# Expert blocks of a transformer layer with scaled float16 high and low parts in place of float32 ones

## The reference

```python
q, k, v = x @ Wq, x @ Wk, x @ Wv                    # 16 heads of 64
a = softmax(q k^T / 8) v;  x = layernorm(x + a @ Wo + bo)
logits = (softmax(q'[:, None] * k'[None, :]) * v').sum()   # 8 experts, q', k', v' = x @ wqkv.T
top 2 of 8 experts per token, weights = softmax of the two logits
h1 = x @ w1[e].T; a, g = split(h1); he = silu(a) * g @ w2[e].T     # a, g: 352 wide
x = layernorm(x + sum of weight * he over the token's two experts)
```

## Time and profile before

| | us |
|---|---|
| median of 3 runs | 823.8 (823.46 to 823.82) |
| the profiled execution | 824.94 |
| its span, first to last instruction | 823.0 |
| PE busy | 761.4 |
| ACT busy | 703.2 |
| POOL busy | 650.7 |
| DVE busy | 532.5 |

### The profile page before, as it was taken

The page is one execution under the profiler, slowest core; times in us unless marked ns, Lnnn a source line. Parts: engine busy times, 40 slices in busy tenths (PEclk is TensorE's granted clock), DMA queues, the critical chain, the costliest instruction groups (busy, mean ns, idle before and its releaser), DMA issues. The chain is left out here.

```text
span 823.0 us, 22272 instructions
## 1 busy us (share of the span) xinstructions
PE 761.4 (93%) x9183; PEld 522.9 (64%) x9183; DVE 532.5 (65%) x836; ACT 703.2 (85%) x941; POOL 650.7 (79%) x416
## 2 busy tenths in 40 slices
PE   1899999999999999999999999999999987999991
PEld 0346565666666666666666666666665656899990
DVE  6857666666666666666686766776666678653453
ACT  3799998989898989899999999998989995566672
POOL 5788897878787878788899878999999981267741
PEclk9999999999999999999999999999999999899995
DMA  5602139303030303030304040404030015113312
GB/s 182 157 2 45 38 72 160 73 11 77 7 69 15 71 12 78 5 79 6 78 5 113 5 114 5 116 2 116 3 82 8 11 34 122 45 40 98 108 40 90
DMA packets 42930, 49.30 MB, mean 60 GB/s; under 512 B 6577, under 2 KB 27447, under 8 KB 42704
## 3 DMA queue, kind: packets, MB, share of 16 engines
q1 hardware_dynamic: 39664, 43.31, 22.4%
q0 software_dynamic: 2496, 4.24, 1.6%
q10 hardware_dynamic: 672, 0.33, 0.2%
HBM read 14.28 MB, written 9.25 MB: 29 GB/s over the span
## 5 line engine op out<-in xcount | busy, mean ns | idle before, releaser
L909 POOL TENSOR_TENSOR pl<-p,ph 128x1024 f16<-128x1024 f32 x242 | 511.4, 2130 | 72.0 <-ACT ph L805 71.8
L972 DVE TENSOR_REDUCE mx<-mps 128x1 f32<-128x1024 f32 x249 | 303.9, 1221 | 132.8 <-PE mps L637 130.6
L804 ACT ACTIVATE p<-sps,escale 128x1024 f32<-128x1024 f32 x256 | 287.4, 1123 | 43.4 <-PE sps L617 36.6
L805 ACT ACTIVATE ph<-sps,escale 128x1024 f16<-128x1024 f32 x256 | 286.2, 1118 | 0.0
L715 PE MATMUL pair_bank<-v,ph 128*128 128x65 f16 x2048 | 214.5, 193 | 5.0 <-DVE ao L1012 4.3
L715 PEld LDWEIGHTS pair_bank<-v,ph 128*128 128x128 f16 x2048 | 190.8, 96 | 39.8 <-DVE pl L976 4.1
L717 PE MATMUL pair_bank<-v,ph 128*128 128x64 f16 x2048 | 214.3, 195 | 0.0
L719 PE MATMUL pair_bank<-v,pl 128*128 128x65 f16 x2048 | 213.9, 192 | 0.0
L717 PEld LDWEIGHTS pair_bank<-v,ph 128*128 128x128 f16 x2048 | 190.0, 97 | 29.0 <-issue 0.2
L616 PE MATMUL sps<-q_hh,k_hl 128*128 128x512 f16 x512 | 194.9, 381 | 3.4 <-ACT ph L805 3.1
L617 PE MATMUL sps<-q_lm,k_h 65*128 65x512 f16 x512 | 195.4, 382 | 0.0
(11 more groups left out here) (249 smaller groups left out, 971.0 us busy)
## 6 DMA issues: line engine op xcount, KB each, us to landing
q_hh<-work SPq DMA_DIRECT2D x60, 128.0 KB, 2.3
k_hl<-work SPq DMA_DIRECT2D x58, 128.0 KB, 2.5
q_lm<-work SPq DMA_DIRECT2D x30, 128.0 KB, 2.4
k_h<-work SPq DMA_DIRECT2D x30, 128.0 KB, 2.5
sorted<-pad SPq DMA_DIRECT2D x1, 2990.0 KB, 17.8
xb<-sorted SPq DMA_DIRECT2D x46, 65.0 KB, 2.1
v<-in_w1T SPq DMA_DIRECT2D x8, 352.0 KB, 3.7
v<-home SPq DMA_DIRECT2D x4, 512.0 KB, 4.5
```

The costliest lines, as they stand in the source:

```text
L804: nc.scalar.activation(p32[:, n % 4, :], sps[:, n % 2, :], ACT.Exp, bias=EXP_BIAS, scale=escale[:, 0:1])
L805: nc.scalar.activation(ph[:, n % 4, :], sps[:, n % 2, :], ACT.Exp, bias=EXP_BIAS, scale=escale[:, 0:1]).then_inc(s_exp, 1)
L909: nc.gpsimd.tensor_tensor(pl[:, n % 4, :], p32[:, n % 4, :], ph[:, n % 4, :], ALU.subtract).then_inc(s_subp, 1)
L972: nc.vector.tensor_reduce(mx[:, i // TB, i % TB:i % TB + 1], src, AX.X, ALU.max).then_inc(s_mx, 1)
```

## The change

The token rows, the gated middle rows and both expert weights are held as a float16 high part and a float16 low part, scaled by fixed units and by the weights' greatest values. Where before tokens and w1 were fp32r halves and the middle rows and w2 plain float32, now all are float16 pairs:

- **Greatest values.** SP loads w1 a second time, as 128 long rows (`w1_raw`), at the end of its part for pair 0, into the tail of the values' tile, and w2 (`w2_raw`) at the end of pair 3. VectorE reduces them in twelve pieces of 704 columns at the slots of `WEIGHT_TOPS`, the first eight waiting for w1_raw. The column of ones in tiles 10 to 15 of the values is set after that. Two jobs are added, `wtop` at (8, 0) and `wspread` at (8, 15), by which the values reach all partitions, and VectorE derives five units from them (seven small instructions).
- **w1, w2.** High parts by ScalarE with a scale, low parts by VectorE as scale times value minus high. w2 is loaded in pair 13; its three high parts are made at ScalarE's start of the mixture, its three low parts (1024 columns each) on VectorE behind `split_block(3)`.
- **Middle rows.** They are cut in 117, 117 and 118 in place of 128, 128 and 96. ScalarE makes the high part of all 384 columns in one instruction; VectorE makes the low part from the bank. `down` has nine float16 products of 128 columns.
- **Order.** ScalarE's `take_hidden(i - 1)` stands ahead of `take_block(i + 2)`; VectorE's `low_hidden(i - 1)` stands between `gated(i)` and `split_block(i + 2)`.
- Rows are scaled by 2048 when they are copied, and the units are taken out in the silu's scale and in the tokens' weights (one more small instruction in `total`). `bo` lies in a part of `ao`. The second batch's value tiles are made tile by tile.

```diff
+WEIGHT_TOPS = {(0, 13): 0, (0, 14): 1, (1, 1): 2, (1, 2): 3, (1, 6): 4, (1, 10): 5, (1, 11): 6, (1, 14): 7,
+               (4, 2): 8, (4, 6): 9, (4, 10): 10, (4, 14): 11}
+FRONT_JOBS = {(8, 0): ("wtop", 0), (8, 15): ("wspread", 0), (9, 15): ("turnx", 0), ...
-F_CHUNKS = [(0, 128), (128, 128), (256, 96)]
+F_CHUNKS = [(0, 117), (117, 117), (234, 118)]
...
@@ sync, in the loop over pairs, behind spread_head @@
+                if pp == 0:
+                    sp.dma_start(f.w1_raw, io["w1T"].rearrange("e h f -> (e h f)").rearrange(
+                        "(p n f) -> p n f", p=P, n=8)).then_inc(f.s_w1raw, 16)
+                if pp == 3:
+                    sp.wait_ge(f.s_wtops, 8)
+                    sp.dma_start(f.w2_raw, ...).then_inc(f.s_w2raw, 16)
+                if pp == 13:
+                    for c, (off, n) in enumerate(F_CHUNKS):
+                        sp.dma_start(f.w2[0:n, :, c, :], ...).then_inc(f.s_w2, 16)
...
@@ vector, attention @@
+                if kind == "wspread":
+                    then = lambda ins: f.then(dve, "vector", ins)
+                    nc.vector.tensor_scalar(f.bound, misc[:, 0:2], 1.0 / W_TOP, 1e-30, ALU.mult, ALU.max).then_inc(s_used, 1)
+                    dve.wait_ge(s_used, job + 1)
+                    then(nc.vector.reciprocal(f.scale, f.bound))
+                    then(nc.vector.tensor_scalar(f.he_unit, f.scale[:, 0:1], HE_UNIT, None, ALU.mult))
...
+            def top_of_weights(k):
+                dve.wait_ge(f.s_w1raw if k < 8 else f.s_w2raw, 16)
+                part = f.w1_raw[:, k, :] if k < 8 else f.w2_raw[:, k - 8, :]
+                nc.vector.tensor_reduce(f.tops[:, k:k + 1], part, AX.X, ALU.max,
+                                        apply_absolute_value=True).then_inc(f.s_wtops, 1)
...
@@ vector, loop over steps, behind reduce_max and the step's job @@
+                    if (pp, s) in WEIGHT_TOPS:
+                        top_of_weights(WEIGHT_TOPS[pp, s])
...
@@ tensor, down @@
-                    mm = nc.tensor.matmul(y_bank, heT[0:n, i % 2, c * P:(c + 1) * P], w, start=(c == 0),
-                                          stop=(c == len(F_CHUNKS) - 1))
+                    nc.tensor.matmul(y_bank, high, w_hi, start=(c == 0), stop=False)
+                    nc.tensor.matmul(y_bank, high, w_lo, start=False, stop=False)
+                    mm = nc.tensor.matmul(y_bank, low, w_hi, start=False, stop=(c == len(F_CHUNKS) - 1))
...
@@ scalar, mixture @@
-                nc.scalar.copy(heT[:, i % 2, 0:2 * P], heT_bank[:, 0:2 * P])
-                nc.scalar.copy(heT[0:F - 2 * P, i % 2, 2 * P:], heT_bank[0:F - 2 * P, 2 * P:]).then_inc(s_heT, 1)
+                nc.scalar.activation(heT_hi[0:FC, i % 2, :], heT_bank, ACT.Copy, scale=f.he_unit[0:FC]).then_inc(s_heThi, 1)
...
+                if i < B * NBB + 1:
+                    take_hidden(i - 1)
                 if i + 2 < B * NBB:
                     take_block(i + 2)
-                if i < B * NBB + 1:
-                    take_hidden(i - 1)
                 weigh(i - 2)
...
@@ vector, mixture @@
+            def low_hidden(i):
+                dve.wait_ge(s_heThi, i + 1)
+                nc.vector.scalar_tensor_tensor(out=heT_lo[0:FC, i % 2, :], in0=heT_bank, scalar=f.he_unit[0:FC],
+                                               in1=heT_hi[0:FC, i % 2, :], op0=ALU.mult,
+                                               op1=ALU.subtract).then_inc(s_heT, 1)
...
             for i in range(2, B * NBB):
                 gated(i)
+                low_hidden(i - 1)
                 if i + 2 < B * NBB:
                     split_block(i + 2)
```

More of the change, by code:

```diff
@@ L27 @@
 XW_TOP = 16384.0
+X_UNIT = 2048.0
+W_TOP = 32768.0
+HE_UNIT = 2.0 ** -40
+BACK_UNIT = 2.0 ** 29
 MAX_UNIT = 32768.0
@@ L126, in value_tile @@
 def value_tile(j):
-    batch, j = divmod(j, 2 * TB)
+    if j >= 2 * TB:
+        return TB + (j - 2 * TB) // 2, j % 2
     h, i = divmod(j, TB)
-    return batch * TB + i, h
+    return i, h
 class Front:
@@ L141, in __init__ @@
         self.w1 = first_values[:, 0:end].bitcast(F32).rearrange("p (e f) -> p e f", e=E)
-        self.w1_lo = first_values[:, 0:end].bitcast(F32R).rearrange("p (e f) -> p e f", e=E)
-        self.w1_hi = work[:, 0:end].bitcast(F32R).rearrange("p (e f) -> p e f", e=E)
+        half = 2 * E * F
+        self.w1_hi = work[:, 0:half].rearrange("p (e f) -> p e f", e=E)
+        self.w1_lo = work[:, half:2 * half].rearrange("p (e f) -> p e f", e=E)
+        self.w2_hi = work[:, 2 * half:2 * half + 3 * E * D].rearrange("p (e c d) -> p e c d", e=E, c=3)
+        self.w2 = sb("w2", [P, E, 3, D], F32)
+        raw = v[:, T * H * VW - 2 * E * 2 * F:].bitcast(F32)
+        self.w1_raw = raw.rearrange("p (n f) -> p n f", n=8)
+        self.w2_raw = raw[:, E * 2 * F - E * F:].rearrange("p (n f) -> p n f", n=4)
+        ws = sb("ws", [P, 32], F32)
+        self.tops, self.top = ws[:, 0:12], ws[:, 12:14]
+        self.bound, self.scale = ws[:, 14:16], ws[:, 16:18]
+        self.he_unit, self.silu_unit, self.back_unit = ws[:, 18:19], ws[:, 19:20], ws[:, 20:21]
+        self.highest, self.spread_top = ws[0:2, 21:22], ws[0:2, 22:24]
         self.x1T = first_values[:, end:end + 2 * S].bitcast(F32)
@@ L341, in front_part @@
         dst = f.rows[b][:, slot, 4 * half:4 * half + 4, 0:D]
-        last = nc.scalar.copy(dst, src) if name == "scalar" else unit.tensor_copy(dst, src)
+        last = nc.scalar.activation(dst, src, ACT.Copy, scale=X_UNIT)
     if kind == "multiply":
@@ L397, in front_part @@
         then(unit.tensor_reduce(one[:, 4], g[:, 6], AX.X, ALU.add))
-        last = unit.reciprocal(one[:, 3], one[:, 4])
+        then(unit.reciprocal(one[:, 3], one[:, 4]))
+        last = unit.tensor_scalar(one[:, 3], one[:, 3], f.back_unit, None, ALU.mult)
     if kind == "share" and k == 1:
@@ L785, in _ @@
                             value += 1
+                        if kind == "wtop":
+                            pe.wait_ge(f.s_wtop, 2)
+                            pe.wait_ge(s_used, j)
+                            nc.tensor.transpose(misc[0:2, 0:P], f.top, mem["ident"][:]).then_inc(s_misc, 1)
+                        if kind == "wspread":
+                            pe.wait_ge(f.s_const, FRONT_CONSTANTS)
+                            pe.wait_ge(f.s_wscale, 1)
+                            pe.wait_ge(s_used, j)
+                            nc.tensor.matmul(misc[:, 0:2], f.ones[0:2, :], f.spread_top, start=True,
+                                             stop=True).then_inc(s_misc, 1)
                         if kind == "turnx":
@@ L897, in _ @@
                             act.wait_ge(s_head[a], spreads(a, PAIRS))
-                        nc.scalar.copy(f.w1_hi[:, e, :], f.w1[:, e, :]).then_inc(f.s_w1hi, 1)
+                        act.wait_ge(f.s_wscale, 2)
+                        nc.scalar.activation(f.w1_hi[:, e, :], f.w1[:, e, :], ACT.Copy,
+                                             scale=f.scale[:, 0:1]).then_inc(f.s_w1hi, 1)
                     front_at(nc, act, "scalar", f, pp, s)
@@ L1017, in take_front @@
                 dve.wait_ge(s_misc, job + 1)
+                if kind == "wtop":
+                    nc.vector.tensor_reduce(f.highest, misc[0:2, 0:P], AX.X, ALU.max).then_inc(s_used, 1)
+                    dve.wait_ge(s_used, job + 1)
+                    nc.vector.tensor_scalar(f.spread_top, mem["ident"][0:2, 0:2], f.highest, None,
+                                            ALU.mult).then_inc(f.s_wscale, 1)
+                if kind == "wspread":
+                    then = lambda ins: f.then(dve, "vector", ins)
+                    nc.vector.tensor_scalar(f.bound, misc[:, 0:2], 1.0 / W_TOP, 1e-30, ALU.mult, ALU.max).then_inc(s_used, 1)
+                    dve.wait_ge(s_used, job + 1)
+                    then(nc.vector.reciprocal(f.scale, f.bound))
+                    then(nc.vector.tensor_scalar(f.he_unit, f.scale[:, 0:1], HE_UNIT, None, ALU.mult))
+                    then(nc.vector.tensor_scalar(f.silu_unit, f.bound[:, 0:1], 1.0 / X_UNIT, None, ALU.mult))
+                    then(nc.vector.tensor_scalar(f.back_unit, f.bound[:, 0:1], BACK_UNIT, None, ALU.mult))
+                    then(nc.vector.tensor_scalar(f.back_unit, f.back_unit, f.bound[:, 0:1], None, ALU.mult))
+                    nc.vector.tensor_scalar(f.back_unit, f.back_unit, f.bound[:, 1:2], None, ALU.mult).then_inc(f.s_wscale, 1)
+                    dve.wait_ge(f.s_wscale, 2)
                 if kind == "turnx":
@@ L1317, in take_block, with high_second @@
                 nc.scalar.copy(x_hi[:, i % 2, :], x_of(i)).then_inc(s_xhi, 1)
+            def high_second(c):
+                n = F_CHUNKS[c][1]
+                act.wait_ge(f.s_w2, 16 * len(F_CHUNKS))
+                nc.scalar.activation(w2_hi[0:n, :, c, :], f.w2[0:n, :, c, :], ACT.Copy,
+                                     scale=f.scale[0:n, 1:2]).then_inc(s_w2hi, 1)
+            high_second(0)
             take_block(0)
+            high_second(1)
```

(6 more changed lines are left out.)

77 lines of the change are left out of this document (52 added, 25 removed).

## The result

| | kernel before | changed kernel |
|---|---|---|
| median, us | 823.63 (4 runs, 823.2 to 823.8) | 862.98 (4 runs, 861.6 to 864.3) |
| ratio | 1 | 1.0475, 95% interval 1.0453 to 1.0497 |
| span of the profiled execution | 823.0 | 861.8 |
| mean granted clock | 0.981 | 0.973 |

The change makes the kernel slower by 39 us, where 16 were forecast. Of the 38.8 us of the spans, 16.2 arise in attention (forecast 13.7) and 22.5 in the mixture (forecast 2.4).

A forecast was written before the change was run, and what follows sets the result against it. TensorE's pace was taken to bound the attention loop, VectorE blocks 2 to 9, and a ring the later blocks. Terms 10.1 + 1.9 + 1.7 - 1.1 + 3.2 + 0.3 = +16.1 gave 840 us as median, range 830 to 848.

The forecast's parts named there:

- The stall: Attention, slot (0, 13): VectorE waits for the w1_raw load and TensorE behind it, +10.1 us.
- Rivals B: Attention: the w1 load is as slow as the 17.8 us transfer, stall 19 instead of 10, 849 us; chance 0.10.
- D: Attention: the wait for w1_raw is not paid because its load is under way earlier, 828 us; chance 0.05.
- The clock: Attention, behind the pause: TensorE's clock falls at least once, +1.9 us (bounds 0 and 3.7).
- The units at (9, 0): Attention, step (9, 0): VectorE's seven small dependent instructions land nearly wholly on TensorE, +1.7 us (bounds 0 and 2.5).
- The job at (8, 0): Attention, slot (8, 0): two small VectorE instructions in an empty step, cost 0.
- The other eleven weight reductions: Attention: VectorE's further reductions of raw weights are hidden by its idle time, cost 0, +1 kept for the range.
- The late blocks: Expert blocks from i = 10 on: cheaper products give pauses and hardly any time, 37 x 0.03 = -1.1 us.
- TensorE alone: Expert blocks: without waits for other engines, TensorE's period falls from 2.07 to 1.93 or 1.84 us.
- the ring: Expert blocks: chain from TensorE through ScalarE and VectorE's low part and x_lo to the next turn, 2.06 us (bound 2.15).
- Rival A: Expert blocks run at TensorE's pace, from block 10 on -8.5 instead of -1.1, 833 us; chance 0.17.
- The early blocks and the start: Mixture through block 9: VectorE is the bound and its added low parts cost +3.2 us (bounds 1.5 and 5).

The follow-up runs named there:

- e4: Changed kernel with w1_raw issued right behind wqkv, both jobs at (8, 3) and (8, 9), a second token bank, expert numbers loaded four at a time: 855.23 us, ratio 1.037.
- c5: Changed kernel with w1 and w2 read at fixed places, no register load, and a second bank for turned tokens: 849.10 us, period 2.235, most 1.93.
- c2: Changed kernel with w1 and w2 read at fixed places and no register load of the expert: 849.51 us, period 2.264.
- d1: Changed kernel with float32 down products, w1_raw issued early, the two jobs moved, old block order, one load a block: 827.65 us, ratio 1.0056, period 2.094.
- a1: Changed kernel with only the w1_raw load issued earlier, right behind the wqkv load: 880.12 us, ratio 1.038, period 2.544.
- c4: Kernel before with the register load of the expert done twice from block 10 on: 843.29 us, period 2.695.
- c3: Changed kernel with the register load of the expert done twice from block 10 on: 886.58 us, period 3.178.
- e2: Changed kernel with float32 down products, w1_raw issued early, jobs moved, old block order, expert numbers loaded four at a time: 840.64 us, ratio 1.019, period 2.419.

## Why the prediction was right or wrong

- **The stall: right.** 10.1 forecast, 11.1 measured at the first reduction behind it. The transfer took 9.6 us from issue to landing, 8.8 forecast. In the two microseconds from 88 on the DMA engines moved 439 GB/s, more than the 358 GB/s of the Trainium skill (DMA: Bandwidth & Descriptors, the summary of limits), as the 414 of the earlier trace rows had said. Rivals B (19 us) and D (no wait) are out.
- **The clock: right in the main.** 1.9 forecast; step (1, 0) is 12.85 late, of which 11.1 is the pause, so 1.7. The second weight reduction has no part in it: it ends at 96.96, and the maxima reduction behind it starts at 97.30, when TensorE's slow product (1.03 us for the 0.60 of the earlier trace rows) is done. The granted clock averages 0.54 from 88 to 90 us, when TensorE had stood still since 85.6, and is 0.50, the lower of the two levels, from 94 to 101. One support of the forecast was weaker than it looked. The earlier trace rows give durations and no clock: the 512-column products do follow each other 0.43 us apart until 20.82 and 0.22 from 21.17 on, but the row of 17 to 21 us has the granted clock 1.00, so that the lower level there was read from the spacing alone.
- **The units at (9, 0): right,** 1.7 forecast, 1.46 measured.
- **The job at (8, 0): wrong, +1.3 where 0 stood.** I costed its two instructions. What it did was make (8, 0) a slot with a job, and in such a slot the low half of the values goes ahead of the reduction, which then waits for ScalarE. In e4, with the job at (8, 3), the reduction comes first again and (8, 1) follows 4.55 us behind (7, 15), as before; here 5.86.
- **The other eleven weight reductions: nearly right,** 0 forecast. 12.9, 1.3 and 1.5 are 15.6 of the 16.2 us that attention lost; the 0.6 left I have not placed.
- **The late blocks: wrong, and this is the step that failed.** "TensorE alone: 2.07 - 0.14 = 1.93 us, or 1.84" was about right: the products and turns of the changed kernel stand 1.86 us from end to end (766.35 to 768.15, and 0.06), and c5 has 1.93, with 0.06 more ahead of its middle rows' turn. "Sum 0.60 + 0.04 + 0.49 + 0.03 + 0.46 + 0.29 + 0.15 = 2.06" is the right ring in the right order, and 2.25 in c2: heT_hi comes 0.67 behind the turn (0.64 forecast), heT_lo 0.62 behind that (0.52), x_lo 0.53 behind that (0.46) and the next turn 0.43 (0.44). The new forms are dearer than the plain ones I took them from:

```profile
L1534 DVE SCALAR_TENSOR_TENSOR heT_lo<-bank,ws,heT_hi 118x384 f16<-118x384 f32 x35 | 21.5, 615 | 0.0
L1421 ACT ACTIVATE heT_hi<-bank,ws 118x384 f16<-118x384 f32 x35 | 20.1, 574 | 0.9 <-PE bank L1324 0.9
L1415 ACT ACTIVATE silu<-bank,ws 128x352 f32<-128x352 f32 x35 | 19.4, 554 | 38.7 <-PE bank L1316 38.7
```

  574 ns for the 490 forecast, and the silu 554 where it was 462 without its scale from memory. But neither number sets the time. The claim that fell is "So the cheaper products give TensorE pauses and hardly any time": it took array and ring for the only two limits. (Its 0.03 a block goes by the 2.04 of quick signals; by its own 2.06 it is 0.01, and from i = 10 on there are 36 blocks and not 37. That changes the sum by under 1 us.) The sequencer, which I did not price at all, has 2.55, so 35 blocks cost 15.5 us where -1.1 stood. Rival A, that the blocks run at TensorE's pace, named the right engine and the wrong part of it.
- **The early blocks and the start: too small,** 3.2 forecast, 5.8 measured (1.2 + 4.6). In c2, without register instructions, blocks 2 to 10 take 25.2 instead of 26.2, so the sequencer has 1.0 of it. The rest fits the low halves on VectorE: d1, without those of the middle rows and of w2, takes 22.1 against 21.6 before.
- **The tail: too small,** 0.3 against 1.2; no run looked at it.
- The range ended at 848: it held the ring's bound (2.15) and not a third limit.

The rows held a hint. TensorE had no pause in the blocks before, and a unit with no pause can be fed just in time or with a lot to spare; busy rows don't say which. Six products, and five address instructions of which no row shows a duration, had gone at nothing beyond their array time. Taken with what the runs give, 0.05 for an address instruction (0.29 / 6, at least) and 0.074 for a register operation, five more and two fewer are +0.10. Of the 0.44 us between the periods that leaves up to 0.34 for the six products more of the program's list, which are three matmuls with three weight loads in the trace: 0.11 for such a pair. That is an estimate from differences. No run took products away by themselves; d1, which takes away these three pairs and three address instructions, also opens the ring and changes the order, and is 0.45 under a1. The Trainium skill (TensorE: Matmul & The Clock Gate, the section "Wait — 56ns, not 53.3ns?") gives some 62 ns of sequencer time to a matmul where it isn't decoded by hardware, and calls this the bound once the array's work is shorter. By it three more matmuls would be an estimated 0.19 us a block, 46 times, 9 us: half of what I missed. No run here shows whether matmuls are decoded so on this chip: 24 of them follow each other 0.03 us apart from 64.72 to 65.46 in the trace before (the first are in the earlier trace rows), but they may have been issued ahead.

## What to carry to other kernels

Where blocks are worked with register addresses, count what the engine's sequencer has to do for a block, beside what the array does: loads of registers first (0.6 us each here, with their bounds), then address and register instructions (0.05 to 0.07), then the products themselves. Splitting three float32 products into nine short float16 ones, each with addresses of its own, can make the array's time shorter and still lose. To see it, look for an idle stretch whose named releaser was done long before, with the weight load waiting for "issue"; to prove it, double a load whose value nobody uses. And an edit that only adds a job to a slot can change the order of everything that asks whether the slot has one.

## What the hardware showed that I had not expected

- One more load into a TensorE register, with its two bounds instructions, lengthened a block by 0.58 to 0.63 us in c4 and c3, though its result is not needed. One instruction that fills four registers left TensorE idle for 1.5 us in e2.
- The kernel before, with TensorE at 73.6 of 73.6 us, had some 0.04 us a block left in the sequencer, if a load costs the same there as in the changed kernel: two limits within 2% of each other.
- With its scale read from memory a silu of 352 columns takes 554 ns, 462 without.
- A faster block can run into its own data: c5 waited 3.79 us for results on their way home and gave back what the open ring had brought.
